# Loading the identity and beta first, and the other constants earlier, in a four-layer graph kernel

## The reference

```
x = layernorm(x + gnn0(x, adj))
x = layernorm(x + gnn1(x, adj))
x = layernorm(x + gnn2(x, adj))
x = layernorm(x + gnn3(x, adj))

gnn0: inv_deg = 1 / (sum(adj, axis=1) + beta)
      agg = adj @ x + beta[:, None] * x
      return inv_deg[:, None] * agg @ kernel + bias
gnn1: three rounds of relu(adj @ (h @ W) + b), then relu(h + x)
gnn2: d^-1/2 adj d^-1/2 @ (x @ W + b), with d = sum(adj, axis=1)
gnn3: softmax((x W_l)(x W_r)^T) @ x @ W_h @ W_g * gamma + adj @ x
```

## Time and profile before

| what | us |
|---|---|
| median of 3 runs | 1361.51 |
| lowest and highest of the 3 | 1359.14, 1367.57 |
| the profiled execution | 1359.1 |
| its span, first to last instruction | 1357.3 |
| TensorE busy | 1291.2 (95%) |
| VectorE busy | 929.9 (69%) |
| ScalarE busy | 716.5 (53%) |
| GpSimd busy | 255.3 (19%) |

### The profile page before, as it was taken

How to read it: one execution, slowest core, us unless ns; L and a number is a source line. 1 busy time by engine, 2 the same in 40 slices (tenths; PEclk the granted TensorE clock), 3 DMA queues, 4 the chain that set the end, 5 groups by cost and what they waited for, 6 DMA issues and landing times.

```text
span 1357.3 us, 17259 instructions
## 1 busy us (share of the span) xinstructions
PE 1291.2 (95%) x5911; PEld 795.1 (59%) x5911; DVE 929.9 (69%) x1213; ACT 716.5 (53%) x880; POOL 255.3 (19%) x167
## 2 busy tenths in 40 slices
PE   8799999998999988899999999999899999999987
PEld 3344444433333232588888788887567767767764
DVE  5466665561000164799999988886988888878885
ACT  0211010112111032588888777776788788787785
POOL 0111001100000011001010100005243343344345
PEclk9899999998999999999999999999999999999999
DMA  9586655553979989899999999990000000000000
GB/s 374 203 338 247 234 224 207 205 203 131 369 302 377 359 285 407 300 358 374 375 380 376 333 356 360 385 355 0 1 1 0 1 1 1 0 18 15 0 1 31
DMA packets 81087, 288.01 MB, mean 212 GB/s; under 512 B 9466, under 2 KB 11130, under 8 KB 81018
## 3 DMA queue, kind: packets, MB, share of 16 engines
q1 hardware_dynamic: 78768, 286.30, 55.6%
q10 hardware_dynamic: 2250, 0.82, 0.2%
HBM read 284.98 MB, written 2.10 MB: 212 GB/s over the span
## 4 chain that ended last, share of the span: by engine, by line
PE 69%; DVE 13%; issue 6%; ACT 5%; DMA 3%; ACTq 1%; SPq 1%; POOL 1%; DVEq 0%; POOLq 0%
PE acc L1256 14%; PE acc L1324 8%; PE acc L1445 7%; DVE t_lo L989 7%; PE acc L1363 4%; PE acc L1358 4%; PE acc L1359 4%; DMA raw<-in_adj_s 2%; PE rs L1264 2%; PE acc L1435 2%; PE acc L1436 2%; PE acc L1439 2%; PE rs L1329 2%; PE e L1400 2%; PE e L1402 2%
## 5 line engine op out<-in xcount | busy, mean ns | idle before, releaser
L989 DVE TENSOR_TENSOR t_lo<-raw,t_hi 128x1024 fp32r<-128x1024 f32 x256 | 307.4, 1243 | 23.9 <-ACT t_hi L711 18.9
L711 ACT ACTIVATE t_hi<-raw 128x1024 fp32r<-128x1024 f32 x256 | 262.8, 1055 | 39.5 <-PE acc L1363 37.8
L1358 PE MATMUL acc<-t_hi,st_hi 128*128 128x512 f32 x512 | 202.5, 396 | 2.4 <-ACT t_hi L711 2.0
L1359 PE MATMUL acc<-t_hi,st_lo 128*128 128x512 f32 x512 | 199.6, 390 | 0.0
L584 POOL TENSOR_TENSOR ring_lo<-ring,p_hi 128x1024 fp32r<-128x1024 f32 x64 | 155.4, 2428 | 220.4 <-ACT p_hi L765 220.3
L1256 PE MATMUL acc<-raw,x 128*128 128x512 f32 x400 | 179.8, 598 | 0.0
L1363 PE MATMUL acc<-t_lo,st_hi 128*128 128x512 f32 x512 | 159.9, 393 | 5.3 <-DVE t_lo L989 5.0
L1063 DVE TENSOR_TENSOR ring<-ring,e 128x1024 f32<-128x1024 f32 x128 | 153.9, 1211 | 0.1
L759 ACT ACTIVATE ring<-ring 128x1024 f32<-128x1024 f32 x128 | 134.2, 1054 | 25.0 <-DVE ring L1063 24.9
L1256 PEld LDWEIGHTS acc<-raw,x 128*128 128x128 f32 x400 | 74.0, 191 | 92.3 <-issue 92.3
L556 POOL COPY x<-xn 128x512 f32<-128x512 f32 (+1 forms) x24 | 20.7, 864 | 565.0 <-ACT xn L652 565.0
(11 more groups left out here) (214 smaller groups left out, 1878.1 us busy)
## 6 DMA issues: line engine op xcount, KB each, us to landing
raw<-in_adj_s SPq DMA_DIRECT2D x506, 512.0 KB, 5.8
kept_t<-in_adj_s SPq DMA_DIRECT2D x8, 512.0 KB, 7.4
x<-in_x SPq DMA_DIRECT2D x4, 512.0 KB, 10.2
kept_x<-in_adj_s SPq DMA_DIRECT2D x4, 512.0 KB, 6.6
kept_e<-in_adj_s SPq DMA_DIRECT2D x4, 512.0 KB, 7.6
kept_l<-in_adj_s SPq DMA_DIRECT2D x4, 512.0 KB, 7.2
kept_s<-in_adj_s SPq DMA_DIRECT2D x4, 512.0 KB, 7.0
kept_v<-in_adj_s SPq DMA_DIRECT2D x4, 512.0 KB, 7.3
```

Source lines behind the costliest of these rows:

```text
L711: nc.scalar.activation(t_hi[:, g % HL, :], raw[:, k, :], ACT.Copy).then_inc(hi_done, 1)
L989: nc.vector.tensor_tensor(t_lo[:, k, :], raw[:, slot_no(s, c, g), :], t_hi[:, k, :].bitcast(F32), ALU.subtract).then_inc(lo_done, 1)
L1358: mm(a[:, :], block_of(st_hi, b), hi[:, m], start=(g == 0 and j == 0), stop=False)
L1359: mm(a[:, :], block_of(st_lo, b), hi[:, m], start=False, stop=False)
```

## The change

`ident` and `beta` leave the list `consts` and form a list `consts_first` with a semaphore of its own, `first_in`. ScalarE issues these two at once, without a wait. The other 16 are issued when the second quarter of x has landed (`x_in[1]`), no longer the fourth (`x_in[3]`). The waits for the first `bx` and for the first multiplication by the identity are for `first_in`. The wait for `const_in` stands now at GpSimd's first `xb` and at TensorE's first `epilogue_1`. VectorE's wait in `degrees` stays as it is.

```diff
-        consts = [(ident, ident_in), (comb, comb_in), (k0, w["L0_gnn_kernel"]), (w1, w["L1_gnn_W1"]),
+        consts_first = [(ident, ident_in), (beta, beta_in)]
+        consts = [(comb, comb_in), (k0, w["L0_gnn_kernel"]), (w1, w["L1_gnn_W1"]),
...
-                  (gamma, w["L3_gnn_gamma"].partition_broadcast(P)), (beta, beta_in)]
+                  (gamma, w["L3_gnn_gamma"].partition_broadcast(P))]
...
         def _(pool):
-            pool.wait_ge(const_in, n_const)
+            pool.wait_ge(first_in, 16 * len(consts_first))
             pool.wait_ge(x_all, XP)
...
                 alone(pool)
+                if s == 0 and first(c):
+                    pool.wait_ge(const_in, n_const)
                 if s == 0:
                     nc.gpsimd.tensor_tensor(blocks(xb[:, :]), blocks(cols(x, c)), over_blocks(bias0[:, :]),
...
-            act.wait_ge(x_in[XP - 1], 16)
+            for dst, src in consts_first:
+                nc.scalar.dma_start(dst[:, :], src).then_inc(first_in, 16)
+            act.wait_ge(x_in[1], 16)
             for dst, src in consts:
                 nc.scalar.dma_start(dst[:, :], src).then_inc(const_in, 16)
...
             def epilogue_1(s, c, par):
                 pe.wait_ge(S["at"], done("at", s, c))
                 if s == 0:
+                    if first(c):
+                        pe.wait_ge(const_in, n_const)
...
                 if c == 0:
-                    pe.wait_ge(const_in, n_const)
+                    pe.wait_ge(first_in, 16 * len(consts_first))
```

More of the change, by code:

```diff
@@ L242, in build @@
         past_wait = sem("past_wait")
+        first_in = sem("first_in")
         const_in, memset_done, out_done = sem("const_in"), sem("memset_done"), sem("out_done")
```

## The result

The changed kernel takes 1350.93 us (median of 7 runs, 1348.34 to 1353.86), the kernel before 1359.14 us in the same comparison (7 runs). The ratio is 0.9932, 95% interval 0.9911 to 0.9952, or 9.2 us less with 6.5 to 12.1 as its interval (the two medians alone lie 8.2 us apart). The forecast was 1350.7 us within 1346.5 to 1356.

What follows compares the result with a forecast made beforehand. TensorE, busy for 1291.2 of 1357.3 us, was taken as the bound. From the profiled execution, 1359.1 - 8.73 - 1.14 + 0.3 = 1349.5 us; from the median, 1351.9; the middle, 1350.7, was forecast, range 1346.5 to 1356.

Steps and rivals of the forecast that it cites:

- The wait: End of row 0: `bx` is done by 31.7 us, ahead of TensorE at 35.54, so its whole 8.73 us wait goes.
- The clock: Behind the wait for `bx`: TensorE no longer pauses, so the work at the lower clock goes too, 1.14 us.
- The start: First tile: identity and beta beside the first transfers delay TensorE's start, 0.3 us lost, between 0 and 1.0.
- Earlier constants against tiles: Row 0: 16 constants share the DMA engines with tiles, whose lead covers it; cost 0, bad end 0.6 us.
- rival 1: Row 0: constants starve the tiles and TensorE stops for 2.8 us, 1352.3 to 1354.7; chance 0.14 together with a late `bx`.
- The moved waits: `const_in` at L1171 and GpSimd's first `xb`: constants land at 29.8 to 31.1, some 9 us ahead of L1171; cost 0.
- The rest moves up as a whole: After row 1: transfers wait for free slots and nothing for an absolute time, so the later program keeps the gain.
- rival 3: A later sweep: DMA is the bound and the earlier start ends in another wait, 1359 to 1361; chance 0.04.
- The number: Whole kernel: forecast 1350.7 us, within 1346.5 to 1356; the forecast case had chance 0.80.
- base: Starting time for the 9.57 us gain: profiled execution 1359.14 or median 1361.51, giving 1349.5 or 1351.9; the middle was taken.
- Within 1%: Whole kernel: the measured time differs from the kernel before by less than about 13.6 us; chance 0.86.

Runs made afterwards that it cites:

- The controls: Variants of either kernel with identity and beta issued at the start or later; TensorE starts at 6.43 to 6.56 us with them at the start.
- quarter_only: Kernel before, with all 18 constants in one list with one semaphore, issued behind the second quarter of x; ratio 0.9981.
- again: The changed kernel run and profiled once more, with no edit; ratio 0.9919 to the kernel before.
- split_only: Changed kernel, with the 16 other constants waiting for the last quarter of x again, identity and beta still first; ratio 0.9938 to the kernel before.
- bx_late_14: Changed kernel, with GpSimd repeating row 0's `bx` 14 more times so that it is ready late; ratio 1.0030 to the kernel before.
- bx_late_7: Changed kernel, with GpSimd repeating row 0's `bx` 7 more times so that it is ready late; ratio 0.9981 to the kernel before.

## Why the prediction was right, point by point

*The wait.* The 8.73 us are gone, as worked out. `bx` ended at 27.99; the bound was 31.7. The 2.97 us between the copies and `bx` before were beta's landing, not GpSimd's own start, which is 0.15 us. The 16 issues ended at 19.8 in place of 21.2 to 22.5, mainly since one of them, that of `bias_l`, took 0.47 us in place of 1.42.

*The clock.* The term was 1.14 us. The same stretch now takes 6.03 against 7.48 us, so it was 1.45 us. I had compared with row 1, whose 6.34 us hold some time of its own.

*The start.* The term was 0.3 us lost. This profile has 0.44, and the controls leave anything from 0 to 0.3, so the term is neither shown nor refuted. A second part I had not counted: the first 16 records took 9.10 against 8.66 us. The controls say that this is chance. The first tile of the row behind, tile 4, starts 0.88 us later in all (15.66 against 14.78). The terms measured make 8.73 + 0.16 + 1.45 - 0.88 = 9.46 us, where 0.16 us are the overlap of L1291 with the modelled end of the matmul ahead of it (15.66 + 20.76 = 36.42 against 36.26); the prediction had 9.57.

*Earlier constants against tiles.* VectorE began with tiles 8 and 12 at 19.75 and 27.25, inside what was forecast, and no matmul of row 0 waits for a tile. The cost is 0, as taken; rival 1 did not come.

*The moved waits: this step failed.* I carried the 18.1 us from first issue to last landing over to the earlier time and got 29.8 to 31.1, and so a cover of 9 us at L1171. Measured are about 36 and 4.6 us (L1171 starts at 40.59). The error was to take the time as a property of the transfers. It is one of the packets and of how full the other queue is: in the kernel before, the last packets went alone, when SP's queue had run dry (728 packets to 91 of SP's in 40 to 43.5 us); in the changed one they take turns with tiles to the end. It cost nothing here, because the cover was large enough. But it led me to call the split needless, and `quarter_only`, of which I expected 9 to 10.5 us, brought 1.21. So the mechanism held for the path that the kernel takes, and the error lay in a step that had room to spare.

*The rest moves up as a whole.* The lead is 9.46 at 42 us and 9.46 at 76.14 (85.60 before). In sweep 1 it is 9.11 (VectorE's `at` of the last row at 373.29 against 382.40). Then this execution loses 3.25 us in one place. In the changed kernel the next `at` are

```profile
373.29 0.69 DVE L863 COPY at<-acc 128x512 f32<-128x512 f32 x1 [13.71 <-PE acc L1332]
...
381.28 0.69 DVE L861 TENSOR_TENSOR at<-acc,sums 128x512 f32<-128x512 f32 x1 [7.30 <-PE acc L1332]
387.86 0.69 DVE L861 TENSOR_TENSOR at<-acc,sums 128x512 f32<-128x512 f32 x1 [5.89 <-PE acc L1332]
```

and before:

```profile
382.40 0.69 DVE L857 COPY at<-acc 128x512 f32<-128x512 f32 x1 [13.63 <-PE acc L1324]
...
388.01 0.69 DVE L855 TENSOR_TENSOR at<-acc,sums 128x512 f32<-128x512 f32 x1 [4.92 <-PE acc L1324]
393.72 0.69 DVE L855 TENSOR_TENSOR at<-acc,sums 128x512 f32<-128x512 f32 x1 [5.02 <-PE acc L1324]
```

The first step took 7.99 us against 5.61 and the second 6.58 against 5.71; the lead is 5.86 behind them. TensorE stops twice there in both kernels, for 0.83 and 0.77 us. Behind it the granted clock of the changed kernel falls:

```profile
375.00:380.00 5.00, 4.23 (x21) 2.13 (x24) 0.00 (x0) 1.39 (x3) 0.00 (x0) 0.61 0.72 284
380.00:385.00 5.00, 5.00 (x28) 1.04 (x22) 0.69 (x1) 0.68 (x1) 0.00 (x0) 0.70 0.14 42
```

and that of `again`, the same program, does not:

```profile
375.00:380.00 5.00, 4.23 (x34) 1.88 (x34) 0.69 (x1) 1.39 (x3) 0.00 (x0) 1.00 0.66 261
380.00:385.00 5.00, 5.00 (x36) 2.05 (x38) 0.45 (x1) 0.92 (x2) 0.00 (x0) 1.00 0.64 210
```

Over the twelve profiles the first step took 5.6 us in five (the kernel before, `again`, `split_only`, `bx_late_14`, `bx_late_7`) and 7.25 to 8.0 us in seven, with waits of any length at 36 us in both groups. Both steps together cost 3.25 us more than before in five of the seven and 1.65 in two. So rival 3, a gain given back later, is not what is seen; a toss of the clock is. Some more goes near the end of sweep 3: the lead falls from 9.64 to 8.30 in `again` (8.6 in the span) and from 6.15 to 5.29 in the changed kernel (5.3 in the span). The runs do not settle what that is.

*The number.* Sum 1349.5, base chosen midway, 1350.7; measured 1350.93. That they agree to 0.2 us is luck: the gain was forecast at 9.57 and measured at 9.2 with 6.5 to 12.1 as its interval, and single executions of one kernel spread over 2 to 13 us here. The base was the larger risk. Within 1% was the likeliest case, and it came.

## What to carry to other kernels

A load that one consumer needs early should have a semaphore of its own; behind a shared one it lands with the last packet of the list, however early it is issued. For small loads beside a full queue, count packets, not bytes. And when a stall of TensorE goes, price it as the wait plus a part for the clock (1.4 to 2.9 us here, behind waits of 2.8 us and more; nothing behind the one of 1.16 us).

## What the runs showed of the hardware

- Turns between the two queues, 386 packets to 384 in 4 us, with packets of ScalarE's queue eight times smaller in bytes (0.18 MB to 1.40). With one semaphore, an issue 12 us earlier brought a landing 2.6 us earlier.
- The clock fell behind a wait of 2.81 us, and in seven of twelve profiles behind two gaps of 0.83 and 0.77 us; behind a wait of 1.16 us it stayed up. One place in a program cost 3.25 us in one execution and nothing in the next.
- An issue on ScalarE's queue took 0.33 to 1.4 us, and the same 16 issues took from 7.4 us (`split_only`) over 9.5 (before) to 10.4 (`quarter_only`).
- GpSimd's `bx` took up to 1.90 us while VectorE was adding tiles and 1.04 us while it was not; VectorE's adds took 1.86 us on average beside it, against 1.37.
